# A mixture-of-experts and attention kernel: the first unit's prologue with its low halves moved from GpSimd to VectorE and behind the one-hot rows

## The reference, cut to what matters

```
x = x + 0.5 * ffn(layernorm(x))
x = x + attn(layernorm(x))
x = x + 0.5 * ffn(layernorm(x))

ffn:  probs = softmax(x @ Wr)             # 8 experts
      the two best experts of each token; the position of a token in its
      expert's queue = how many tokens of its sequence chose it earlier;
      positions from 40 on are dropped
      buf[e, b, pos] = x                  # a gather: 8 experts x 40 slots
      h = relu(buf @ W1[e] + b1[e]);  y = h @ W2[e] + b2[e]
      out = sum over the two choices of p * y[e, b, pos]
attn: 16 heads of 16 features, value width 8; weights (q.k)**2 with a causal
      mask, divided by their sum; then @ Wo
```

## Time and profile before

| what | us |
|---|---|
| median of 3 executions | 198.77 |
| lowest and highest | 197.93 and 199.7 |
| the profiled execution, whole | 198.15 |
| its span in the trace | 196.4 |
| PE busy in the span | 182.0 (93%) |
| ACT busy in the span | 153.6 (78%) |
| DVE busy in the span | 142.9 (73%) |
| POOL busy in the span | 68.2 (35%) |

### The profile page before, as it was taken

One profiled execution on the slowest core, in us unless ns is written; L12 is line 12 of the kernel. 1 busy time (PEld: TensorE's weight loads), 2 busy tenths in 40 slices (PEclk: granted clock), 3 DMA queues, 4 the chain that ended last, 5 costly groups with the idle time before them and its releaser, 6 DMA issues.

```text
span 196.4 us, 6048 instructions
## 1 busy us (share of the span) xinstructions
PE 182.0 (93%) x2329; PEld 145.4 (74%) x2329; DVE 142.9 (73%) x408; ACT 153.6 (78%) x361; POOL 68.2 (35%) x104
## 2 busy tenths in 40 slices
...
DMA packets 21742, 19.69 MB, mean 100 GB/s; under 512 B 1705, under 2 KB 18641, under 8 KB 21713
## 3 DMA queue, kind: packets, MB, share of 16 engines
...
q10 hardware_dynamic: 144, 0.00, 0.0%
...
## 4 chain that ended last, share of the span: by engine, by line
PE 77%; DVE 14%; ACT 3%; issue 2%; POOL 2%; DVEq 0%; ACTq 0%; POOLq 0%
PE psB L993 19%; PE psB L1063 7%; PE psS L1046 4%; PE psS L870 4%; PE psS L871 4%; PE psS L872 4%; PE psB L880 4%; PE psB L969 3%; PE psB L1065 3%; PE psB L951 3%; PE psB L929 3%; DVE xn L711 2%; DVE oh L783 2%; PE psB L1002 2%; PE psB L1084 2%
## 5 line engine op out<-in xcount | busy, mean ns | idle before, releaser
L550 POOL TENSOR_SCALAR_AFFINE_SELECT amat<-amat 128x512 f32<-128x512 f32 x64 | 44.4, 702 | 36.7 <-ACT amat L631 35.3
L631 ACT ACTIVATE amat<-psS 128x768 f32<-128x768 f32 x64 | 48.9, 813 | 3.7 <-PE psS L1048 3.2
L602 ACT ACTIVATE hid<-psS,biasT 128x160 f32<-128x160 f32 x128 | 39.4, 405 | 6.0 <-PE psS L872 5.5
L993 PE MATMUL psB<-hid,w 128*128 128x160 f32 x256 | 40.4, 304 | 0.1
L993 PEld LDWEIGHTS psB<-hid,w 128*128 128x128 f32 x256 | 35.6, 190 | 0.7 <-issue 0.4
L870 PE MATMUL psS<-xe,w 128*128 128x160 f16 x128 | 27.2, 232 | 1.1 <-ACT biasT L582 0.9
L872 PE MATMUL psS<-xe,w 128*128 128x160 f16 x128 | 27.2, 233 | 0.0
L871 PE MATMUL psS<-xe,w 128*128 128x160 f16 x128 | 27.2, 233 | 0.0
L1063 PE MATMUL psB<-amat,vst 128*32 128x256 f32 x256 | 20.4, 389 | 0.2 <-POOL amat L550 0.2
L610 ACT ACTIVATE yT<-psB,biasT 128x160 f32<-128x160 f32 x32 | 12.2, 408 | 7.0 <-PE psB L993 7.0
L711 DVE TENSOR_SCALAR xn<-x,meanvar,rstd 128x128 f32<-128x128 f32 x40 | 15.9, 459 | 0.4
...
## 6 DMA issues: line engine op xcount, KB each, us to landing
...
```

The costliest lines, as they stand in the source:

```text
L550: pool.affine_select(out=d, in_=d, pattern=[[0, 2], [0, 2], [1, P]], compare_op=ALU.is_ge, fill=0.0, base=0, channel_multiplier=-1).then_i ...
L602: ins = act.activation(hid[:, n % 2, c, :], psS[:, wide_slot(s) + c // 2, (c % 2) * GS:(c % 2 + 1) * GS], ACT.Relu, bias=biasT[:, e * HC + ...
L631: act.activation(amat[:, n % A_RING, :, :], psS[:, wide_slot(s):wide_slot(s) + 2, 0:T + P], ACT.Square)\
L993: ins = mm(bank(s)[:, 0:GS], w2[:, e, c, :], hid[:, n % 2, c, :], start=(c == 0), stop=(c == HC - 1))
```

## The change

It has six parts, all of which begin in the prologue of unit (0,0):

1. The low half of the first eight token tiles is made by DVE instead of POOL. The new function `low_half(p)` is called for p = 0 ahead of `key` and for p = 1 between the second and the third one-hot piece.
2. POOL makes no low half of W1 ahead of the one-hot pieces: it waits for `oh_ready` first, then does expert 0, expert 1, the small router matrix, experts 2 to 7.
3. The raw scores are no longer copied to `lg`. DVE takes maximum and difference straight from PSUM, for each half by itself.
4. ACT copies the transposed raw tokens in two pieces of 256 columns, and PE begins the scores behind the first piece (`raw_copied`).
5. The idle products are 6, 56 and 12 instead of 6, 30, 10 and 8, and the second of the later groups stands ahead of the first `dph`.
6. The stage tables are rewritten from end to end. In unit (0,0) `dpl.0.0.2` and `dpl.0.0.3` go from ACT to DVE, `bt` moves ahead of `dph.0.0.3`, `ln1.0.2` moves behind the one-hot pieces, `wr` moves from ACT's second place to behind them, and `w1.1` to `w1.4` go later on ACT. After unit (0,0) the stages are the same and many stand a place or two away from where they stood.

```diff
-ON_SCALAR = {..., ("dpl", 0, 0), ("dpl", 1, 0),
+ON_SCALAR = {..., ("dpl", 0, 0, 0), ("dpl", 0, 0, 1), ("dpl", 1, 0),
...
-wc rx.0 warm.6.0 rx.1 rl.0 rl.1 warm.30.1 warm.10.2 ps.0.0 dph.0.0.0 dpl.0.0.0 warm.8.3 dph.0.0.1 dpl.0.0.1
+wc rx.0 warm.6.0 rx.1 rl.0 rl.1 warm.56.1 ps.0.0 warm.12.2 dph.0.0.0 dpl.0.0.0 dph.0.0.1 dpl.0.0.1 dph.0.0.2
...
+        mean_made, raw_copied = sem("mean_made"), sem("raw_copied")
...
-            for p in range(2):
-                pool.wait_ge(first_hi, p + 1)
-                parts = token_parts(0, p)[0]
-                pool.tensor_tensor(parts[:, 1], xn[:, p], parts[:, 0], ALU.subtract).then_inc(first_split, 1)
-            pool.wait_ge(wsm_hi, 1)
-            pool.tensor_tensor(wsm[:, 1, WR], wsml[:, WR], wsm[:, 0, WR], ALU.subtract).then_inc(wsm_split, 1)
+            pool.wait_ge(oh_ready, GB)
             for e in range(E):
-                if e == 2:
-                    pool.wait_ge(oh_ready, GB)
                 pool.wait_ge(w1_hi, e + 1)
                 pool.tensor_tensor(w1[:, 1, e, :], ...).then_inc(w1_split, 1)
+                if e == 1:
+                    pool.wait_ge(wsm_hi, 1)
+                    pool.tensor_tensor(wsm[:, 1, WR], wsml[:, WR], wsm[:, 0, WR], ALU.subtract).then_inc(wsm_split, 1)
...
-                    act.activation(xr[:, p, :], bank(s), ACT.Copy).then_inc(taken(s), 1)
+                    w = PTT * P // 2
+                    act.activation(xr[:, p, 0:w], bank(s)[:, 0:w], ACT.Copy).then_inc(raw_copied, 1)
+                    act.activation(xr[:, p, w:], bank(s)[:, w:], ACT.Copy).then_inc(taken(s), 1)
...
+            def low_half(p):
+                dve.wait_ge(first_hi, p + 1)
+                parts = token_parts(0, p)[0]
+                dve.tensor_tensor(parts[:, 1], xn[:, p], parts[:, 0], ALU.subtract).then_inc(first_split, 1)
...
-                    ins = dve.tensor_copy(lg[:, PTT * p:PTT * (p + 1), :],
-                                          bank(s)[:, 0:PTT * E].rearrange("p (t e) -> p t e", e=E))
+                    raw = bank(s)[:, 0:PTT * E].rearrange("p (t e) -> p t e", e=E)
+                    q = slice(PTT * p, PTT * (p + 1))
+                    link(dve.tensor_reduce(lmax[:, q], raw, AX.X, ALU.max))
+                    if p:
+                        wait_taken(dve, ("rl", 0))
+                    ins = dve.tensor_tensor(ldiff[:, 0, q], raw, lmax[:, q]..., ALU.subtract)
                     ins.then_inc(taken(s), 1)
-                    if p:
-                        wait_taken(dve, s)
-                        link(dve.tensor_reduce(lmax[:, :], lg[:, :, :], AX.X, ALU.max))
-                        dve.tensor_tensor(ldiff[:, 0], lg[:, :, :], over_experts(lmax), ALU.subtract).then_inc(diff_ready, 1)
...
                 elif kind == "ps":
+                    if n == 0:
+                        low_half(0)
                     wait_ready(dve, s)
...
                     for i in range(GB):
+                        if n == 0 and i == GB // 2:
+                            low_half(1)
                         dve.tensor_tensor(
...
                 elif kind == "rl":
...
-                    wait_taken(pe, ("rx", p))
                     for t in range(PTT):
+                        if t == 0:
+                            pe.wait_ge(raw_copied, p + 1)
+                        elif t == PTT // 2:
+                            wait_taken(pe, ("rx", p))
```

More of the change, by code:

```diff
@@ L127 @@
+up.1.0.2 down.1.0.1 up.1.0.3 down.1.0.2 ot.1.0.0 up.1.0.4 ot.1.0.1 ot.1.0.2 up.1.0.5 down.1.0.3 up.1.0.6
+ot.1.0.3 down.1.0.4 down.1.0.5 up.1.0.7 down.1.0.6 dph.1.1.0 dph.1.1.1 dph.1.1.2 dph.1.1.3 ex.1.1 up.1.1.0
+up.1.1.1 down.1.0.7 down.1.1.0 yt.1.0.0 up.1.1.2 up.1.1.3 yt.1.0.1 yt.1.0.2 down.1.1.1 up.1.1.4 down.1.1.2
+up.1.1.5 down.1.1.3 down.1.1.4 up.1.1.6 up.1.1.7 yt.1.1.0 down.1.1.5 down.1.1.6 down.1.1.7 yt.1.1.1 yt.1.1.2
+yt.1.1.3
 """)
 DVE_STAGES = stages("""
-wc ln1.0.0 ln1.0.1 rl.0 nm.0.0 nm.0.1 rl.1 c1.0.0 c2.0.0 ln1.0.2 ps.0.0 lnx.0.2 ln2.0.2 ln1.0.3 xt.0.2 lnx.0.3
```

117 lines of the change are left out of this document (58 added, 59 removed).

## The result

| | median us | lowest to highest | executions |
|---|---|---|---|
| before | 198.24 | 197.93 to 201.87 | 9 |
| after | 200.57 | 199.11 to 204.65 | 9 |

The ratio is 1.0087, with a 95% interval of 1.0054 to 1.0119. The changed kernel is slower, by 1.7 us, where a median of 196.4 was forecast. A few executions ran 3 to 5 us longer than the others of the same kernel (here one of before and two after); the ratios leave them out and compare the means of the rest (200.2 and 198.5), while the medians, over all, lie 2.3 us apart. The profiled execution of the changed kernel took 199.95 us.

The account below looks back on a forecast made before the run. PE, busy 182.0 of 196.4 us, was taken as the bound, with time to win in the prologue. Prologue -3.3, first unit +1.1, rest 0 give -2.2 us: median 196.4, range 195.0 to 198.1.

Parts of the forecast that it names:

- Pieces end at 15.74: Prologue, DVE: the one-hot pieces end at 15.74 instead of 18.53, a sum of -2.79 us.
- The term of the POOL subtraction: Prologue, DVE: without POOL's token half beside it, L752 falls from 1.22 to 0.22 us, minus 1.00.
- First product 2.33 us behind: Prologue: first expert product 2.33 us behind the pieces, at 18.07, 3.3 us earlier; DVE late next, no longer ACT.
- The first unit gives back 1.1 us: Unit (0,0): of the 3.3 us won, 1.1 is given back, leaving -2.2 us at its end.
- The casts on ACT: Unit (0,0): two more casts on ACT, 1.3 us, of which 0 to 1.3 is given back; taken as 1.1.
- the collision term: Unit (0,0), DVE: `lnx.0.3` can meet one or two W1 halves, 1 to 2 us, against 1.3 us of room.
- The rest: I take 0, bounds -0.7 and +0.7.: Behind unit (0,0): the new order changes nothing, within 0.7 us, a tenth of ACT's idle time in the attention.
- Idle products cost nothing: Prologue, PE: the 56 and 12 idle products cost nothing; a kept clock was counted as no gain.
- The third: Rival: W1 late, PE waits 0.9 us for each of experts 2 to 7, 5.4 us in all; 200.9 us, chance 0.06.
- The second: Rival: casts, W1 collisions with `lnx.0.3` and the choice, and new order give back 2.5 of 3.3; 198.0 us, chance 0.27.
- the forecast's own lower end: Whole kernel: lower end of the forecast's case, 196.0 to 197.2 us, which had chance 0.45.
- the first rival: Unit (0,0): gain kept almost whole, ACT's idle time takes the two casts; 195.6 us, chance 0.22.

Follow-up runs that it names:

- e3: Changed kernel, with POOL making the W1 low halves of experts 5 to 7 only behind `lnx.0.3`; 199.01 us, ratio 1.0012 to before.
- e8: Changed kernel with e3's wait, second expert unit and attention in the old order, second layer in the new; 195.68 us, ratio 0.9864 to before.
- e5: Changed kernel with the old order from `ot.0.0.0` on and e3's wait; 195.99 us, ratio 0.9869 to before.
- e1: Changed kernel with the old order from `ot.0.0.0` on, behind the first unit; 197.94 us, ratio 0.9987 to before.
- e4: Kernel before, its prologue and first unit kept, with the new order from `ot.0.0.0` on; 201.64 us, ratio 1.0173 to before.
- e2: Changed kernel with 30 idle products on PE ahead of the wait of `xt.0.3`; 200.84 us, ratio 1.0127 to before.
- e10: Changed kernel with the attention's first half, up to `sc.4.2`, in the old order; 200.36 us, ratio 1.0082 to before.
- e14: Changed kernel, new order up to `ox.4`, then the old order to the attention's end; 199.82 us, ratio 1.0055 to before.
- e7: Changed kernel with only PE's position count `ps.1.0` moved, to behind `sc.7.4`; ratio 1.0236 to before.
- e12: e8 with 30, 10 and 8 idle products instead of 56 and 12; 196.38 us, ratio 0.9875 to before.

## Why the prediction was wrong

The forecast had the changed kernel 2.2 us ahead at the end, and its span is 1.7 us behind, 3.9 us off. By the landmarks the prologue was 0.5 better than forecast (3.8 won, 3.3 forecast), the first unit 1.7 worse (2.8 given back, 1.1 forecast) and the rest 2.7 worse (from -1.0 to +1.7, 0 forecast). Against its steps:

- **Pieces end at 15.74.** Measured 15.28. The term of the POOL subtraction was right to the digit: L758 takes 0.22, minus 1.00. From the earlier trace rows the choice's end came 12.32 - 10.80 = 1.52 us earlier, so 0.52 remain for the scores, where 0.22 was counted and the half-sized maximum given nothing. Choice to pieces: 11.65 - 10.80 = 0.85 against 13.74 - 12.32 = 1.42, minus 0.57 (predicted 0.50). The pieces: 3.63 against 4.79, minus 1.16 (predicted 1.07).
- **First product 2.33 us behind.** Measured 17.59 - 15.28 = 2.31, and DVE's moves were late next, as said: PE waited 1.36 us for them. Won: 3.8 us, where 3.3 was forecast. Part of this agreement is the execution's: e3 and e8, with the same prologue, show 2.9 and 3.2.
- **The first unit gives back 1.1 us.** It gave back 2.8. The casts on ACT were put at 1.1; e3, which has them all, gives back 17.56 - 17.18 = 0.4, and e5, where the clock was also lower, 1.3. So this term was not shown wrong. What failed is the collision term. The collisions with `lnx.0.3` were put at 1 to 2 us and set against 1.3 us of room, so at nothing. L715 lost 1.77 us (2.89 - 1.12) and the cast 0.85 (1.28 - 0.43), 2.6 in all. The room was read at the wrong waiter. The 1.32 us ahead of `key` are DVE waiting for PE's count; but PE needs the step first at `xt.0.3`. There the low half was done at 27.71 before, and the transposes came at 28.48: 0.77 us of room. The two rows of before are

```profile
27.02 0.69 DVE L722 TENSOR_TENSOR xf<-xn,xf 128x512 f16<-128x512 f32 x1
```

```profile
28.48 0.61 PE L929 MATMUL psB<-ident,xf 128*128 128x128 f16 x8
```

  2.6 lost less 0.77 of room is 1.8, and PE stood 1.98. (Counted from the first product, DVE also began the step 0.8 us later than before and PE came to the transposes 0.8 later; these two cancel.) The prediction quoted the Trainium skill's rule ("GPSIMD Engine Reference", section "Key points") as speaking against the change. The trace agrees with it at this place: the normalising step (1.12 to 2.89 us) and the cast with one input (0.43 to 1.28 us) are hit. Whether both ran in a two-port mode no row shows.
- **"The rest: I take 0, bounds -0.7 and +0.7."** This is the step that failed most. The new order behind the first unit costs 2.0 us (e1 against the changed kernel) to 3.4 us (e4), three to five times the bound. Taking a tenth of ACT's idle time as the bound had no row behind it. Sums of idle time don't bound what an order costs: in a stretch in which PE, DVE and ACT each take their list in order, one late choice on DVE stood PE 1.5 us and one late transpose 1.0 us, and both waits are seen in every trace of the unaltered new second half (the changed kernel, e2, e3, e4, e10). With the old one the wait for the choice is gone from every trace; that for the transposes is gone too, but for 0.4 us in e1 and e5. The loss is in this stretch (20.6 us old, 23.5 to 24.1 new), and e14 ties 1.6 to 2.1 us of it to the moves that make the choice late. That the two waits alone are its cause was not isolated: e7, meant for that, brought a wait of its own.
- **Idle products cost nothing.** Not contradicted: e12 against e8 shows no difference beyond the interval, though the clock does follow them.
- **The rivals.** The third, W1 late, gave a time near the measured one (200.9) by luck, for a reason that didn't occur: PE nowhere waited for `w1_split` in the unit. The second named the right collision and a new order that loses a little, and at 198.0 was too mild in both. The slower side got 0.06; its true mechanisms stood in the text as bounds of other cases and had no chance of their own.

With both failed terms taken out, the sum is 3.8 - 0.4 = 3.4 us, or 2.5 with e5's 1.3 for the casts, and e8 keeps 2.7 (0.9864 of 198.46). Its 195.68 lies between the forecast's own lower end and the first rival.
